# VectorE instead of GpSimd copies the index columns of the next turn in the edge passes of a graph kernel

## What is computed

```python
# graph convolution
h = x @ W
deg_inv_sqrt = where(deg > 0, rsqrt(maximum(deg, 1)), 0)
msgs = h[src] * (deg_inv_sqrt[src] * deg_inv_sqrt[dst])[:, None]
x = layernorm(x + segment_sum(msgs, dst))

# three layers, 8 heads of 32
Q, K, V = typed_transform(x, W_Q), typed_transform(x, W_K), typed_transform(x, W_V)   # by node type
kt = typed_transform(K[src], W_E, edge_type)
scores = sum(Q[dst] * kt, -1) / sqrt(32) * mu[edge_type]
w = softmax of scores over the edges of one destination
x = layernorm(x + segment_sum(V[src] * w, dst) @ Wo + bo)
x = layernorm(x + gelu(x @ w1 + b1) @ w2 + b2)
```

## Time and profile before

| | us |
|---|---|
| median of 3 runs | 6563.27 |
| lowest and highest run | 6554.43, 6564.42 |
| span of the profiled execution, first to last instruction | 6558.3 |
| DVE, ACT, PE, POOL busy in that span | 4522.3, 3285.2, 5376.9, 4047.3 |

### The profile page before, as it was taken

The page is one execution under the profiler, slowest core; times in us unless marked ns, Lnnn a source line. Parts: engine busy times, 40 slices in busy tenths (PEclk is TensorE's granted clock), DMA queues, the critical chain, the costliest instruction groups (busy, mean ns, idle before and its releaser), DMA issues. The chain is left out here.

```text
span 6558.3 us, 128194 instructions
## 1 busy us (share of the span) xinstructions
PE 5376.9 (82%) x28010; PEld 4214.7 (64%) x28011; DVE 4522.3 (69%) x11029; ACT 3285.2 (50%) x10707; POOL 4047.3 (62%) x3930
## 2 busy tenths in 40 slices
PE   4566666697888888999888888889997888888897
PEld 3344444496666666788766666668896666666786
DVE  7433333356888888666488888876656888888697
ACT  0333333454666666323466666652244666666443
POOL 0677777546777777233577777743356777777343
PEclk9999999998999999999999999999998999999998
DMA  4444444578777777112887777741168777777111
GB/s 137 123 141 141 140 138 142 154 262 256 233 237 234 234 235 234 31 32 79 275 254 239 234 235 238 236 137 32 32 209 266 236 236 233 238 239 234 38 48 42
DMA packets 574994, 1165.93 MB, mean 178 GB/s; under 512 B 86616, under 2 KB 334128, under 8 KB 574752
## 3 DMA queue, kind: packets, MB, share of 16 engines
q0 software_dynamic: 239984, 774.78, 40.4%
q1 hardware_dynamic: 321359, 377.52, 17.5%
q10 hardware_dynamic: 13536, 12.33, 0.6%
HBM read 966.73 MB, written 204.00 MB: 179 GB/s over the span
## 5 line engine op out<-in xcount | busy, mean ns | idle before, releaser
L1621 POOL DMA_INDIRECT at_kv<-kv_table,at_stage x1664 | 1656.4, 995 | 545.0 <-issue 403.5
L1637 ACT COPY sums<-ps x2499 | 949.8, 380 | 1141.6 <-PE ps L1733 1116.8
L1718 PE MATMUL ps<-at_wv,at_hot 128*128 128x264 f32 x3328 | 1026.7, 403 | 348.5 <-ACT at_hot L1654 194.4
L1621 POOL DMA_INDIRECT at_kv_last<-kv_table,at_stage_last x832 | 824.7, 991 | 273.1 <-issue 205.4
L764 POOL DMA_INDIRECT gc_rows<-x_scaled,gc_stage x832 | 807.4, 970 | 269.9 <-issue 238.3
L1718 PEld LDWEIGHTS ps<-at_wv,at_hot 128*128 128x128 f32 x3328 | 515.1, 191 | 613.7 <-DVE at_wv L1820 354.4
L1733 PE MATMUL ps<-sums,at_hot_t 128*128 x3328 | 873.7, 386 | 26.7 <-DVE at_prod L1802 20.9
L825 PE MATMUL ps<-gc_rows,gc_hot 128*128 128x256 f32 x1664 | 552.4, 428 | 287.3 <-DMA gc_rows<-x_scaled,gc_stage 286.8
L1802 DVE TENSOR_TENSOR at_prod<-ps,at_kv 128x512 f32<-128x512 f32 x832 | 571.5, 687 | 285.5 <-DMA at_kv<-kv_table,at_stage 265.3
L1701 PE MATMUL ps<-zeros_b 128*128 128x264 bf16 x2508 | 695.8, 278 | 32.5 <-PEq L93 19.0
L1733 PEld LDWEIGHTS ps<-sums,at_hot_t 128*128 128x128 f32 x3328 | 579.2, 194 | 188.5 <-issue 19.9
(11 more groups left out here) (411 smaller groups left out, 10812.2 us busy)
## 6 DMA issues: line engine op xcount, KB each, us to landing
kv_table<-pj_v_next SPq DMA_DIRECT2D x98, 396.0 KB, 3.5
kv_table<-pj_k_next SPq DMA_DIRECT2D x98, 384.0 KB, 2.8
at_hot_t<-hot_columns SPq DMA_DIRECT2D x104, 256.0 KB, 4.2
at_kv<-kv_table,at_stage POOLq DMA_INDIRECT x1664, 3.8
at_hot<-hot_rows SPq DMA_DIRECT2D x104, 256.0 KB, 4.8
at_rec<-block_records SPq DMA_DIRECT2D x104, 226.0 KB, 4.1
kv_table<-pj_v SPq DMA_DIRECT2D x49, 396.0 KB, 3.2
kv_table<-pj_k SPq DMA_DIRECT2D x49, 384.0 KB, 2.6
```

Of the source, the lines that this page charges most:

```text
L1621: nc.gpsimd.indirect_dma_start(kv[:, 2 * k + j, :], None, g.tab_d.rearrange("t n c -> (t n) c"), bass.IndirectOffsetOnAxis(index, 0)).then ...
L1637: act.copy(dest, source).then_inc(evacuated, 1)
L1718: mm = t.matmul(own[j], hot[:, slot % HRING, j, :], wv[:, slot % WRING, j, :], start=False, stop=True, skip_group_check=True)
```

## The change

In every edge pass the copy of the index columns moves from GpSimd to VectorE. VectorE copies the columns of turn 0 ahead of its first turn, and those of turn i + 1 in turn i: in the convolution in step 2, behind the copy-out of duo 0 (`LAG_COPY = 2`), in the layers in step 3, behind the product of keys and queries of duo 0 (`LAG_SCORE = 3`). GpSimd keeps the wait on `staged` and the 32 transfers of a turn. So that the half of `stage` is a constant in the code, VectorE's loop now holds two turns: turns 0 and 1 are written out, the loop runs over turns 2 to 23 in 11 passes, and turns 24 and 25 (and 26 in the layers) are written out.

```diff
--- before.py
+++ after.py
@@ -661,12 +661,16 @@
         end_phase(nc, sems)
 
 
-def gather_tiles(nc, pool, idx, stage, staged, used, fetch):
+def stage_indices(v, idx, stage, r, half, staged):
+
+    return v.tensor_copy(stage[:, half, :], idx[:, bass.ds(2 * RING * r, 2 * RING)]).then_inc(staged, 1)
+
+
+def gather_tiles(nc, pool, stage, staged, used, fetch):
 
     def turn(i, half):
         r = 2 * i + half
         first = isinstance(r, int) and r == 0
-        nc.gpsimd.tensor_copy(stage[:, half, :], idx[:, bass.ds(2 * RING * r, 2 * RING)]).then_inc(staged, 1)
         need_apart(pool, staged, r + 1)
         for k in range(RING):
             if not first:
@@ -765,7 +769,7 @@
                         rows[:, (2 * k + j) * D:(2 * k + j + 1) * D], None, g.xs_d,
                         bass.IndirectOffsetOnAxis(index, 0)).then_inc(g.landed[k], 16)
 
-                gather_tiles(nc, pool, g.idx_x, stage, staged, (summed,), fetch)
+                gather_tiles(nc, pool, stage, staged, (summed,), fetch)
 
             @block.scalar
             def _(act):
@@ -912,21 +916,28 @@
                         need(v, hot_t8_stored[b], 16 * i)
                     v.tensor_copy(hot_t8[:, b, u, :], g.ps[:, TRIO[k], 0:GROUP]).then_inc(hot_t8_made, 1)
 
-                def turn(i):
+                def turn(i, half):
                     for k in range(RING):
                         make_hot(i, k)
                         if k >= LAG_COPY:
                             copy_columns(i, k - LAG_COPY)
-                        elif not isinstance(i, int):
+                        elif not isinstance(i, int) or i > 0:
                             copy_columns(i - 1, RING + k - LAG_COPY)
+                        if k == LAG_COPY and not (isinstance(i, int) and i == TURNS - 1):
+                            stage_indices(v, g.idx_x, stage, i + 1, 1 - half, staged)
                         if k == AT_ENDS:
                             tile_ends(i)
                         if k == AT_RECORD:
                             record(i)
 
-                turn(0)
-                with v.Fori(1, TURNS) as i:
-                    turn(i)
+                stage_indices(v, g.idx_x, stage, 0, 0, staged)
+                turn(0, 0)
+                turn(1, 1)
+                with v.Fori(1, TURNS // 2 - 1) as i:
+                    turn(2 * i, 0)
+                    turn(2 * i + 1, 1)
+                turn(TURNS - 2, 0)
+                turn(TURNS - 1, 1)
                 for k in range(RING - LAG_COPY, RING):
                     copy_columns(TURNS - 1, k)
 
@@ -1622,7 +1633,7 @@
                         kv[:, 2 * k + j, :], None, g.tab_d.rearrange("t n c -> (t n) c"),
                         bass.IndirectOffsetOnAxis(index, 0)).then_inc(g.landed[k], 16)
 
-                gather_tiles(nc, pool, g.idx_kv, stage, staged, (weighed, weighed_too), fetch)
+                gather_tiles(nc, pool, stage, staged, (weighed, weighed_too), fetch)
 
             @block.scalar
             def _(act):
@@ -1785,7 +1796,7 @@
                     v.wait_ge(merging, b + 1)
                     v.tensor_tensor(to, faded_sums[:], g.sums[:, first:first + UROW], ALU.add).then_inc(merged, 1)
 
-                def emit(k, at, i):
+                def emit(k, at, i, half):
                     score_now, weigh_now = at(LAG_SCORE), at(LAG_WEIGH)
 
 
@@ -1802,6 +1813,8 @@
                         v.tensor_tensor(prod[:, slot % 2].rearrange("p (j c) -> p j c", j=2),
                                         ps[:, TRIO[slot], :].rearrange("p (j c) -> p j c", j=2), keys,
                                         ALU.mult).then_inc(multiplied, 1)
+                    if k == LAG_SCORE and not (isinstance(i, int) and i >= TURNS - 1):
+                        stage_indices(v, g.idx_kv, stage, i + 1, 1 - half, staged)
                     if across:
                         b, par = across
 
@@ -1881,12 +1894,20 @@
                                                scalar=ends_max[:, par, 1:2], in1=top_first[:], op0=ALU.add,
                                                op1=ALU.max).then_inc(tops_ready, 1)
 
-                def turn(i):
-                    steps(i, lambda k, at: emit(k, at, i))
-
+                def turn(i, half):
+                    steps(i, lambda k, at: emit(k, at, i, half))
+
+                stage_indices(v, g.idx_kv, stage, 0, 0, staged)
                 v.memset(ends_max[:], 0.0).then_inc(softened, 1)
                 v.wait_ge(softened, 1)
-                all_turns(v, turn)
+                turn(0, 0)
+                turn(1, 1)
+                with v.Fori(1, TURNS // 2 - 1) as i:
+                    turn(2 * i, 0)
+                    turn(2 * i + 1, 1)
+                turn(TURNS - 2, 0)
+                turn(TURNS - 1, 1)
+                turn(TURNS, 0)
                 add_first(BLOCKS - 1, (BLOCKS - 1) % 2, fade_sums(BLOCKS - 1, (BLOCKS - 1) % 2))
 
         end_phase(nc, sems)
```

## The result

| | before | after |
|---|---|---|
| median, lowest to highest, us | 6563.85, 6554.43 to 6567.25 (4 runs) | 6500.79, 6499.55 to 6503.36 (4 runs) |
| span of the profiled execution, us | 6558.3 | 6498.6 |
| ratio of the times, 95% interval | | 0.9909, 0.9895 to 0.9923 |

The account below looks back on a forecast made before the run. The edge passes were taken to be bound by POOL's issue of gathers. 92.1 us off POOL's chain less 0.5 for the hand-over gave 91.6 us, so 6471.7 us against the median 6563.27, 1.4% faster; range 6456 to 6502.

Parts of the forecast that it names:

- What goes: POOL's copy and extra gap at 25 boundaries per edge pass: 19.7, 47.0 and 23.4 us, plus 2; 92.1 us off.
- The 0.03 us a gather: The gather behind each copy on POOL lasts 0.98 us, not 0.95; up to 3 us saved, 2 taken.
- What comes, on VectorE: 104 index copies of 0.18 us on VectorE, covered by its 124 us of landing waits a layer; cost nothing.
- a gather of 0.95 us every 1.25 us: POOL's issue rhythm in the edge passes: 832 gathers and their gaps fill the pass, not held up by the ring.
- 5.1 us in hand: Layers' busiest step: VectorE's weighing ends 5.1 us before POOL's gather fills the slot it frees; a 0.2 us copy fits.
- `staged`: POOL's wait for VectorE's copy: nothing except at pass starts, -0.4 to +0.8 us a pass; +0.5 us taken in all.
- the port: VectorE's copies could hold up POOL's gathers at the shared port: 0 taken, up to 19 us kept for the range.
- the loop: VectorE's two-turn loop: 0.3 us seen before a block, at most 4.7 us a branch, under 5.1; cost 0.
- The first: Rival: the 0.9 us gap at POOL's turn boundaries stays, only the copies go: 26 us, 6538 us; chance 0.04.
- The second: Rival: VectorE takes over in layers, only the convolution's 20 us stay, 6543 us, 0.04; milder, copies delaying gathers, 6491 us, 0.06.
- The third: Rival: VectorE's doubled loop stops for code at 10 branches a layer pass; gain gone at 8.2 us, 6601 us; 0.04.
- The prediction's own test: The forecast is wrong if POOL's edge passes don't shrink by what the copies and gaps held.

Follow-up runs that it names:

- run 4: Changed kernel, with GpSimd still copying into a spare tile at each turn's head and waiting for it: 6553.74 us, ratio 1.001 to the kernel before.
- run 5: Changed kernel, GpSimd gathering only one tile of each duo from a layer's second turn on, consumers' work full: 6501.88 us, ratio 0.9914 to the kernel before.
- run 6: Kernel before, GpSimd gathering only one tile of each duo from a layer's second turn on, consumers' work full: 6522.04 us, ratio 0.9945.
- run 7: Changed kernel, with TensorE's transposes of a block's scores moved to the head of their step: 6466.8 us, ratio 0.9861 to the kernel before.
- run 11: Changed kernel with transposes first, plus TensorE's product for the block's ends moved ahead of that step's queries: 6445.11 us, ratio 0.9833 to the kernel before.
- run 3: Kernel before with only VectorE's loops of two turns added, the copies staying on GpSimd: 6601.4 us, ratio 1.0084.
- run 1: Changed kernel, with the weighing reading one operand from PSUM instead of SBUF: 6503.56 us, ratio 0.9929 to the kernel before.
- run 12: Changed kernel with TensorE's transposes first and the weighing reading one operand from PSUM: 6472.21 us, ratio 0.9876 to the kernel before.
- run 8: Kernel before, with GpSimd copying the columns itself in two halves, each half a turn ahead: 6512.18 us, ratio 0.9931.
- run 10: Changed kernel with transposes first and only one gather a duo from each layer's second turn on: 6466.28 us, ratio 0.9868 to the kernel before.
- run 9: Kernel before, with only TensorE's transposes moved to the head of their step: 6550.94 us, ratio 0.9998.

## Why the prediction was partly wrong

**What goes: right.** The copies left POOL, and the gap fell to the ordinary 0.30 us at all 100 boundaries. They gave 20.2 us in the convolution (19.7 forecast), 47.7 in layers 1 and 2 (47.0) and 23.7 in the last (23.4). The 0.03 us a gather that was to go besides went too: the gather behind a boundary took 0.97 to 0.98 us before (median of each pass) and takes 0.95 now. In the convolution, by means, it took 1.04 and takes 0.95, 2.3 us in all, which is most of the 3.5 us by which its gathers became shorter.

**What comes, on VectorE: the failed step.** "It is covered. In a layer VectorE idles 124 us for landings", "some 96 are left", "On the path: nothing". That the copies cost next to nothing is right (run 4). Wrong is what the sentence takes the wait for: room for a faster POOL. The consumers' own pace was never priced. In a layer it is 1090 us (runs 5 and 6), and the kernel before stood 14, 13 and 9 us above it, 36 in all. By the same products the layers gave 33 us, by first to last gather 36.3 of the 71.4 that POOL saved, and stopped there; 34 us of the forecast's 70.4 for the layers are missing, and the convolution gave 5 more than its term. A last layer of 1080 us was out of reach until the floor was lowered (runs 7 and 11).

A second term was passed over. The prediction gives POOL "a gather of 0.95 us every 1.25 us", but in the kernel before the gathers of a layer took 991 to 998 ns on average, 34 to 40 us a pass more than 832 of 0.95 us. It took these lengths as fixed, and they are not: they grew by 33.9 us in the three layers, which is where the missing 34 us stand in POOL's account.

Both of the readings used as proof of room failed for the same reason. The 124 us of waits for landings were not spare: once data came sooner, VectorE waited at another place, for the transposes, by nearly the same sum. And the "5.1 us in hand" is the distance between two engines at one step, not a stock from which an engine can make up time. Run 3 shows it most plainly: stops of 4 us, less than the 5.1 in hand, cost their full 40 us in a pass.

**How the loss shows.** It did not show as POOL waiting, which is what the prediction said to look for, because gathers that start while a weighing runs take up to 0.49 us more, and in the changed kernel there are more of these: 233, 228 and 227 in the three layers, before 162, 187 and 189. Take the extra length away, and in run 1 the same time appears as waiting; run 12 has both the short gathers and the waits. Why more of them coincide stays open.

**`staged`, the port, the loop.** In layer 1 the hand-over cost what it should: 1.02 us from VectorE's first instruction to the first gather (1493.36 to 1494.38), 0.1 more than in the earlier trace rows. The convolution's first gather came 4.0 us later, 2.9 of it because the section ahead ended that much later. The other 1.1 us are the hand-over, above the bound of 0.8: there VectorE's copy stands behind two clearings of its own, 1.1 us from the start of the first to the start of the copy. The port cost nothing by the int32 copies, as taken: in the changed kernel 55 of them start inside a gather, and those gathers take 0.942 to 0.949 us. The doubled loop shows at most 0.39 us at a branch in this kernel; the bound of 4.7 us for one branch was near the 3.95 us of run 3, whose longest was 4.3.
The Trainium skill ("Runtime: NRT & Kernel Launch", Instruction fetch mechanics) says that a taken branch outside of the two blocks held stalls; run 3 fits this, with 3.95 us a branch and 130 instruction packets instead of 71, though no run shows which code was held.

**The rivals.** The first, that the gap stays, is refuted by the 0.30 us and by run 8. The second, VectorE takes over, was nearest: the consumers do take over. It even placed the lack at the softmax, where runs 7 and 10 find 11 us of the floor. But its price came from losing the whole gain in the layers, and its sign was to be POOL's waits for the weighing above 0.4 us, which stayed at 0.33. The third did not happen in the changed kernel and is real in run 3; its threshold of 5.1 us is wrong, as stops below it cost their full length there. The prediction's own test, that POOL's passes shrink by what copies and gaps held, failed in the layers. A rival with the floor as its price would have given 6563.3 - 20 - 36 = 6507 us, 6 from what was measured.

## What to carry to other kernels

Before a gain on the producer is priced in full, ask for the consumers' floor: let the producer do half of its work and see what the section takes then; here the gain came to about the distance to that and no further. A wait for data, or a lead of some us between two engines, isn't spare throughput: here the one turned into another wait of nearly the same sum, and the other saved nothing. A change that seems to give too little can gain its rest from the order of a few instructions on an engine that the change does not touch (runs 7 and 11: 0.5% and another 0.2 to 0.3%); the first of these brought nothing in the kernel before (run 9).

## What the runs showed of the hardware

- A gather that starts while VectorE runs a weighing of two operands in SBUF took up to 1.44 us instead of 0.95. With one of them in PSUM no gather that starts while a weighing runs took over 0.96 (mean of all in the last layer 951 ns against 1008). The Trainium skill ("SBUF — State Buffer", Who interferes with whom) says that an instruction of VectorE with two inputs in SBUF contends with one of GpSimd that reads there; these rows agree, if a gather's reading of its row numbers from `stage` is such a read, which no run varied.
- GpSimd, waiting for a copy that it had itself just issued, stood 0.89 us in the convolution, behind a copy of 0.22 us. With the copy made half a turn ahead, 0.38 us lay between the gathers around it instead of 0.30, though the copy itself still took 0.20.
- A copy of 128 x 32 int32 on VectorE (0.17 us) that starts inside a gather did not lengthen it: 55 such gathers took 0.942 to 0.949 us.
- In run 3 the same loop of VectorE, once as shared code of two layers and once as the last layer's copy, took 0.3 to 0.4 us at its branch in the first and 3.95 us in the second.
